# Reordering the opening, attention's last steps and the last stage's first block in a fused conditioned transformer block

## What is computed

```
# layer 0
shift, scale, gate = split(silu(t) @ ada_w + ada_b, 3)
norm = where(mask, layernorm(x) * (1 + scale) + shift, 0)
mlp  = gelu(norm @ ssm_w1 + b1) @ ssm_w2 + b2      # and the same with bwd_*; both summed
x    = x + gate * where(mask, mlp, 0)
x    = x + gate_mlp * (gelu_tanh(mod(layernorm(x)) @ ff_w1 + b) @ ff_w2 + b)
# layer 1
x    = x + attention(mod(layernorm(x)))            # 16 heads of 32, 128 x 128 scores
x    = x + (gelu(mod(layernorm(x)) @ w1 + b1) @ w2 + b2)   # hidden 2048
```

## Time and profile before

| | us |
|---|---|
| median of 3 runs (lowest, highest) | 1960.13 (1960.12, 1961.02) |
| the profiled execution's own time | 1960.09 |
| its span, first to last instruction | 1958.3 |

### The profile page before, as it was taken

How to read it: one execution, slowest core, us unless ns; L and a number is a source line. 1 busy time by engine, 2 the same in 40 slices (tenths; PEclk the granted TensorE clock), 3 DMA queues, 4 the chain that set the end, 5 groups by cost and what they waited for, 6 DMA issues and landing times.

```text
span 1958.3 us, 33154 instructions
## 1 busy us (share of the span) xinstructions
PE 1902.1 (97%) x11210; PEld 1573.8 (80%) x11210; DVE 1226.1 (63%) x2058; ACT 717.5 (37%) x2106; POOL 481.6 (25%) x577
## 2 busy tenths in 40 slices
PE   5999999999999999999999998899999999999999
PEld 4778888887888887888888886678888888888887
DVE  6577777766777765888888888445252534436222
ACT  3222232332232233777777776322121212122111
POOL 4333333322222222334443442101010101002000
PEclk8999999999999999999999999899999999999999
DMA  8545444444445443777777877512020111102000
GB/s 291 202 153 173 152 149 155 156 143 140 156 155 167 165 146 99 231 246 259 254 249 246 263 252 253 178 49 87 1 87 23 63 48 37 64 21 85 0 22 22
DMA packets 225104, 276.40 MB, mean 141 GB/s; under 512 B 15212, under 2 KB 144840, under 8 KB 225032
## 3 DMA queue, kind: packets, MB, share of 16 engines
q1 hardware_dynamic: 210712, 232.16, 35.8%
q0 software_dynamic: 12160, 39.14, 6.5%
q10 hardware_dynamic: 2160, 4.20, 0.6%
HBM read 175.29 MB, written 100.14 MB: 141 GB/s over the span
## 4 chain that ended last, share of the span: by engine, by line
PE 85%; DMA 6%; DVE 4%; issue 2%; ACT 1%; SPq 1%; POOL 1%; ACTq 0%; DVEq 0%; POOLq 0%
PE wide L657 33%; PE banks L634 32%; PE banks L1426 16%; PE wide L1459 2%; DMA turned_squares<-rows 2%; PE spare L1482 2%; DMA rows<-gate_bias_rows 1%; DMA rows<-turned_squares 1%; DMA x_tiles<-turned_probs 1%; DVE rows L893 1%; DMA rows<-in_L_cond_w_dram 1%; DMA turned_probs<-probs_room 0%; ACT probs_room L1621 0%; DVE weights L948 0%; DVE h L920 0%
## 5 line engine op out<-in xcount | busy, mean ns | idle before, releaser
L657 PE MATMUL wide<-weights,h 128*128 128x512 f32 x3072 | 758.8, 397 | 13.2 <-DVE h L920 13.2
L634 PE MATMUL banks<-xn,weights 128*128 128x512 f32 x3048 | 734.2, 391 | 5.6 <-DVE xn L908 5.6
L657 PEld LDWEIGHTS wide<-weights,h 128*128 128x128 f32 x3072 | 578.5, 189 | 155.4 <-DVE h L920 14.3
L634 PEld LDWEIGHTS banks<-xn,weights 128*128 128x128 f32 x3048 | 573.4, 188 | 130.7 <-DVE xn L908 6.0
L791 ACT ACTIVATE rows<-banks,vecs 128x512 f32<-128x512 f32 x256 | 176.4, 689 | 938.6 <-PE banks L634 928.4
L918 DVE CAST h<-rows 128x512 fp32r<-128x512 f32 x256 | 118.9, 464 | 441.0 <-ACT rows L791 439.7
L1426 PE MATMUL banks<-xn,weights 128*128 128x256 f32 (+1 forms) x1524 | 194.9, 289 | 0.7 <-DVE xn L1738 0.7
L1426 PE MATMUL banks<-weights,xn 128*128 128x512 f32 x780 | 189.5, 399 | 5.9 <-DVE xn L1785 5.9
L780 ACT ACTIVATE rows<-rows,mod_tables 128x128 f32<-128x128 f32 x360 | 148.4, 483 | 122.4 <-DMA rows<-turned_squares 121.6
L1426 PEld LDWEIGHTS banks<-xn,weights 128*128 128x128 f32 x1524 | 188.9, 193 | 4.8 <-DVE xn L1738 1.1
L920 DVE TENSOR_TENSOR h<-rows,h 128x512 fp32r<-128x512 f32 x256 | 185.1, 723 | 8.8
(11 more groups left out here) (132 smaller groups left out, 1491.0 us busy)
## 6 DMA issues: line engine op xcount, KB each, us to landing
turned_squares<-rows SPq DMA_DIRECT2D x124, 256.0 KB, 2.8
rows<-turned_squares SPq DMA_DIRECT2D x124, 256.0 KB, 2.9
turned_probs<-probs_room SPq DMA_DIRECT2D x62, 512.0 KB, 3.3
x_tiles<-x SPq DMA_DIRECT2D x98, 256.0 KB, 3.3
x<-x_tiles SPq DMA_DIRECT2D x96, 256.0 KB, 3.5
rows<-gate_bias_rows POOLq DMA_DIRECT2D x64, 256.0 KB, 4.0
probsT_room<-turned_probs SPq DMA_DIRECT2D x64, 256.0 KB, 4.1
x_tiles<-turned_probs SPq DMA_DIRECT2D x64, 256.0 KB, 4.9
```

The lines of the kernel that those rows point to most:

```text
L634: last = nc.tensor.matmul(m1_bank(c), st.tiles[0](a, k, c), xn[:, parity, b, k, :], start=s == 0, stop=s == len(steps) - 1)
L657: last = nc.tensor.matmul(y_ps[:, tile, :], h[:, c % 2, a, tile * P:(tile + 1) * P], st.tiles[1](b, c), start=c == 0 and s == 0, stop=c == ...
```

## The change

In the opening SP loads the tokens before the condition weights, and the weights in eight slices of 128 rows, each with a semaphore that PE waits for as it gets to it. The 15 vectors are loaded from ACT's queue. PE turns the first two token tiles and the vectors ahead of the condition product. DVE normalises all four tiles ahead of the table and splits the first weight pieces ahead of the tokens; POOL splits two pieces and then waits until the tokens are split. In block 0 of the first stage POOL asks for weight piece 2 between the fourth bias row's load and its addition, not behind the addition.

In attention's pair 0 DVE takes the row maxima before it splits the value bias, and SP alternates store and load of the squares. In the last steps SP loads the last pair's first half of probabilities and stores the second before it loads the squares; the store and the residual load of tile 1 go to the end. DVE does `finish(14, 0)` behind the row maxima and `finish(14, 1)` behind the output's split. ACT modulates before it copies the output. PE weighs the last tile between the two chunks ahead.

In the last stage's first block PE runs two first products ahead, in three banks; the last of them uses the bank of the old order. Pieces are split in the steps of `STEP_PIECES`: two in chunk 0, one in each of chunks 1 to 4, two in each of chunks 5 to 9. SP loads three token tiles ahead of the first pieces. One semaphore is made lasting, which changes no order.

```diff
@@ -277,7 +279,10 @@
         y_ps = sh.wide
-        m1_bank = lambda c: sh.banks[:, c % 2, :]
+        in_long_lead = lambda n: second_half_first and isinstance(n, int) and n == 0
+
+        def m1_bank(n, c):
+            return sh.banks[:, c % 3 if in_long_lead(n) and c < chunks - 1 else c % 2, :]
@@ -319,6 +324,9 @@
         LATE_LOAD_STEPS = {1: (2, 3), 3: (4, 5)}
+        STEP_PIECES = [(0, 1), (2,), (3,), (4,), (5,), (6, 7), (8, 9), (10, 11), (12, 13), (14, 15)]
+        step_of_piece = [c for c, pieces in enumerate(STEP_PIECES) for q in pieces]
+        own_pieces = lambda n, c: STEP_PIECES[c] if in_long_lead(n) and c < len(STEP_PIECES) else ()
@@ -379,13 +387,11 @@
                     sp.dma_start(cond, t["cond"]).then_inc(cond_loaded, 16)
-                    load_ada(0)
-                    load_ada(1)
...
                         load_x(stages[0], 0, 0, tile)
-                    for vec_name, (row, count) in VEC_ROWS.items():
-                        vector = t[vec_name][0:count * P].rearrange("(c p) -> c p", p=P)
-                        sp.dma_start(vec_rows[row:row + count, :], vector).then_inc(vec_loaded, 16)
+                    for k in range(KC):
+                        for n in range(2):
+                            sp.dma_start(room.weights[n][:, k, :], ada_items[n][k * P:(k + 1) * P, :]).then_inc(slice_loaded[k], 16)
@@ -396,13 +402,15 @@
                     sp.wait_ge(sh.cleared, 1)
+                    sp.wait_ge(sh.stored["att"][0], 16 * NPAIR)
+                    load_x(stages[0], 1, 1, 0)
+                    sp.wait_ge(*sh.values_read)
+                    for tile in range(TPP):
+                        load_x(stages[0], 1, 1, TPP + tile)
...
                         load_own_piece(q)
-                    for tile in range(TPP):
-                        sp.wait_ge(sh.stored["att"][tile], 16 * NPAIR)
-                        load_x(stages[0], 1, 1, tile)
-                    for tile in range(TPP):
-                        load_x(stages[0], 1, 1, TPP + tile)
+                    sp.wait_ge(sh.stored["att"][1], 16 * NPAIR)
+                    load_x(stages[0], 1, 1, 1)
@@ -415,11 +423,12 @@
                             for q in range(STAGE_RING, len(st.prefetch)):
-                                if tile == max(0, (q - STAGE_RING) // 2 - STATS_STEP + 1):
+                                if step_of_piece[q - STAGE_RING] == tile:
...
                             swap_squares(1, tile)
-                        for q in range(STAGE_RING + 2 * (TPB + STATS_STEP - 1), len(st.prefetch)):
-                            load_own_piece(q)
+                        for q in range(STAGE_RING, len(st.prefetch)):
+                            if step_of_piece[q - STAGE_RING] >= TPB:
+                                load_own_piece(q)
@@ -555,12 +564,12 @@
                 pool.wait_ge(zeroed, 2)
-                rstd_of(0, 0)
-                rstd_of(0, 1)
+                for tile in range(TPB):
+                    rstd_of(0, tile)
                 first_low(1)
-                rstd_of(0, 2)
-                rstd_of(0, 3)
-                for q in range(3, len(first_pieces), 2):
+                first_low(3)
+                pool.wait_ge(xn_ready, TPB)
+                for q in range(5, len(first_pieces), 2):
@@ -590,9 +599,11 @@
                         rstd_of(n + 1, tile + 1)
+                    if room and n == 0 and tile == TPB - 1:
+                        load_piece(stages[0], 2)
...
                 if not second_half_first:
-                    if n + 1 < total:
+                    if n + 1 < total and not (room and n == 0):
@@ -617,7 +628,14 @@
                     pe.wait_ge(xn_ready, ln(TPB * (n + 1)))
-                if not (isinstance(n, int) and n == 0 and c < 2):
+                if in_long_lead(n):
+                    if c == chunks - 1:
+                        pe.wait_ge(act_done, c - 1)
+                    elif c >= 3:
+                        pe.wait_ge(act_done, c - 2)
+                    else:
+                        pe.wait_ge(*sh.products_read)
+                elif not (isinstance(n, int) and n == 0 and c < 2):
@@ -661,9 +679,11 @@
-            def pair_product(out, cond_in, weights):
+            def pair_product(out, cond_in, weights, by_slices=False):
                 for k in range(KC):
+                    if by_slices:
+                        pe.wait_ge(slice_loaded[k], 32)
@@ -689,9 +709,10 @@
             def ada_product(out, pair):
-                pe.wait_ge(ada_loaded[2 * pair], 16)
-                pe.wait_ge(ada_loaded[2 * pair + 1], 16)
-                pair_product(out, room.silu, room.weights[2 * pair:2 * pair + 2]).then_inc(products_done, 1)
+                if pair:
+                    pe.wait_ge(ada_loaded[2 * pair], 16)
+                    pe.wait_ge(ada_loaded[2 * pair + 1], 16)
+                pair_product(out, room.silu, room.weights[2 * pair:2 * pair + 2], by_slices=pair == 0).then_inc(products_done, 1)
@@ -702,24 +723,28 @@
                 nc.tensor.transpose(cond_ps[:, P:P + B], mask_f, sh.ident[0:B, 0:B]).then_inc(mask_turned, 1)
+                first_turn(0)
+                first_turn(1)
+                pe.wait_ge(vec_loaded, 16 * len(VEC_ROWS))
+                nc.tensor.transpose(vec_ps[:, 0:N_VEC], vec_rows[0:N_VEC, :], sh.ident[0:N_VEC, 0:N_VEC]).then_inc(vec_turned, 1)
...
                 ada_product(item_ps, 0)
-                pe.wait_ge(vec_loaded, 16 * len(VEC_ROWS))
-                nc.tensor.transpose(vec_ps[:, 0:N_VEC], vec_rows[0:N_VEC, :], sh.ident[0:N_VEC, 0:N_VEC]).then_inc(vec_turned, 1)
...
                     opening()
-                    for tile in range(TPB):
+                    for tile in range(2, TPB):
...
             def block_step(n, parity, before, st, after):
-                first_product(st, n, parity, 0)
+                lead = 2 if in_long_lead(n) else 1
+                for c in range(lead):
+                    first_product(st, n, parity, c)
                 for c in range(chunks):
-                    if c + 1 < chunks:
-                        first_product(st, n, parity, c + 1)
+                    if c + lead < chunks:
+                        first_product(st, n, parity, c + lead)
@@ -818,28 +843,29 @@
                     act.dma_start(mask_u8[:, :], t["mask"]).then_inc(mask_loaded, 16)
+                    for vec_name, (row, count) in VEC_ROWS.items():
+                        vector = t[vec_name][0:count * P].rearrange("(c p) -> c p", p=P)
+                        act.dma_start(vec_rows[row:row + count, :], vector).then_inc(vec_loaded, 16)
...
                     nc.scalar.activation(room.silu, room.cond, ACT.Silu).then_inc(silu_done, 1)
-                    first_high(0)
-                    first_high(1)
...
                     for tile in range(TPB):
+                        first_high(tile)
                         modulate(stages[0], 0, tile)
-                        if tile in (1, 2):
-                            first_high(tile + 1)
...
                 for c in range(chunks):
-                    if second_half_first and isinstance(n, int) and n == 0 and 2 * c < len(st.prefetch):
-                        for q in (2 * c, 2 * c + 1):
-                            piece_high(st, n, q, st.prefetch[q][1], q % STAGE_RING, q // STAGE_RING)
+                    if in_long_lead(n) and c + 1 < chunks:
+                        activate(st, n, c + 1)
+                    for q in own_pieces(n, c):
+                        piece_high(st, n, q, st.prefetch[q][1], q % STAGE_RING, q // STAGE_RING)
...
                         first_high(11 + 2 * c)
-                    if c + 1 < chunks:
+                    if not in_long_lead(n) and c + 1 < chunks:
@@ -983,10 +1009,10 @@
             def first_table_rows():
+                dve.wait_ge(vec_turned, 1)
+                nc.vector.tensor_copy(sh.vecs[:, :], vec_ps[:, 0:N_VEC]).then_inc(vecs_done, 1)
...
                 nc.vector.tensor_copy(rows, item_ps[:, 0:HALF_D]).then_inc(rows_copied, 1)
-                dve.wait_ge(vec_turned, 1)
-                nc.vector.tensor_copy(sh.vecs[:, :], vec_ps[:, 0:N_VEC]).then_inc(vecs_done, 1)
@@ -1018,18 +1044,14 @@
                         stats(stages[0], 0, 0, tile)
+                    for tile in range(TPB):
+                        normalise(stages[0], 0, 0, tile)
                     first_table_rows()
-                    normalise(stages[0], 0, 0, 0)
                     make_first_table()
-                    normalise(stages[0], 0, 0, 1)
-                    normalise(stages[0], 0, 0, 2)
-                    split_xn(0, 0, 0)
-                    normalise(stages[0], 0, 0, 3)
-                    split_xn(0, 0, 1)
                     first_low(0)
-                    split_xn(0, 0, 2)
                     first_low(2)
-                    split_xn(0, 0, 3)
+                    for tile in range(TPB):
+                        split_xn(0, 0, tile)
@@ -1051,9 +1073,8 @@
```

(28 more changed lines are left out.)

20 lines of the change are left out of this document (12 added, 8 removed).

## The result

The changed kernel takes 1950.91 us (median of five runs, 1947.45 to 1952.47), the kernel before 1960.13; the ratio is 0.9947, with a 95% interval of 0.9937 to 0.9958. That is 9.2 us less where I forecast 16.4: the sign and the range hold, the size doesn't. The profiled execution is the one of 1950.91, its span 1949.1, so the two profiled executions differ by 9.2 us too and can be compared place by place. The ratio goes by all executions of a series; by it the gain is 10.4 us (8.2 to 12.3). Later series of the kernel before, on other chips of this kind, lie between 1956.3 and 1965.5, with medians of 1959.3 to 1961.9. One program on one chip spreads over up to 9 us, so single experiments are compared by their ratios and intervals, and the mechanism is read from the traces.

What follows compares the result with a forecast made beforehand. TensorE, busy 97% of the span, was taken as the bound, gains only where it idles or clocks low: -1.0 - 5.6 + 0 - 4.4 - 5.4 = -16.4, from 1960.1 to 1943.7 us; range 1937 to 1953.

Steps and rivals of the forecast that it cites:

- Opening: Until the first product: tokens loaded first bring it to 28.1 to 28.2 from 29.16, -1.0 us (bounds -2.0 to +1.0).
- Border: Blocks 0 and 1: earlier weight piece 2 cuts PE's idle gap and keeps the clock up, -5.6 us (bounds -3.3, -6.2).
- The clock's 2.3 us: Border of blocks 0 and 1: 12 matmuls no longer run at 1.2 instead of 2.4 GHz, 2.3 us of gain.
- Attention's first pair: Row maxima earlier, but exponentials still wait behind modulate of tile 1: 0 us (bounds -1.1 and +0.5).
- Attention's end: Last pair: probabilities loaded 3.0 us earlier, chunk 1 covers copy and split: -4.4 us (bounds -2.0 and -6.0).
- Rival 2: Attention's end: loads contend with stores, not brought forward; -2.0 for -4.4, whole 1946.1; chance 0.08 outside the forecast's band.
- Last stage: First block: two first products ahead, fewer pieces a step, less idle PE: -5.4 us (bounds -2.4 and -7.5).
- rival 1: Last stage's pieces 0 and 1 land late as today; clock still falls at the border: -11.1, 1949.0; chance 0.17.
- The slower rival: Opening: vector loads wait behind SP's bulk until about 33; table +20, less 15.4 elsewhere: 1964.7 us; chance 0.04.

Runs made afterwards that it cites:

- x_bestv: x_best with the vectors' transpose and copy put back behind the condition product: 1940.09 us, ratio 0.9901.
- x_best: Changed kernel plus four edits: last stage's pieces early, old opening split order, late weights held behind squares, late tables behind block 1's second rstd: 1940.11 us, ratio 0.99.
- x_order: Changed kernel with the old order of splits on ScalarE and VectorE between first table and first product: 1946.72 us, ratio 0.992.
- x_squares: Changed kernel with ScalarE's second pair of late weights held until the squares of block 1's tile 1 have landed: 1949.43 us, ratio 0.9955.
- attention alone: Kernel before with only the new attention orders (first pair and last steps): 1956.07 us, ratio 0.9978.
- x_bias: x_best with block 0's first bias load asked for ahead of weight piece 1: 1938.78 us, ratio 0.989.
- x_tables: Changed kernel with POOL's late tables and their store moved behind the first bias load of block 1: 1950.44 us, ratio 0.9944.
- x_pieces: Changed kernel with the last stage's first four weight pieces asked for ahead of attention's last residual load and last two stores: 1945.05 us, ratio 0.9915.
- opening alone: Kernel before with only the opening's part of the change: 1960.25 us, ratio 0.9997.
- border alone: Kernel before with only the next stage's weight piece 2 asked for ahead of the fourth bias add: 1958.44 us, ratio 0.9987.
- last stage alone: Kernel before with only the last stage's part: two first products ahead, pieces over ten steps, three token tiles loaded first: 1956.38 us, ratio 0.9977.
- x_weights: Changed kernel with ScalarE's issue of the second late-weight pair written behind the modulate of block 1's tile 0: 1951.1 us, ratio 0.9943.

## Why the prediction was right or wrong

**Opening** (forecast -1.0, measured nothing). The term that failed is the last vector: it landed at 12.8, inside the bounds that I gave (9 to 13.7) but not under 12.05, where I took it; the product started at 13.18, not 12.4, and the table was at 18.1, not 17.15. Even that was not all it hung on: x_bestv doesn't wait for the vector, and its product ends only 0.3 us earlier than that of x_best. Token tile 2 landed only at 7.1, where I had all four by 6.2, but that cost nothing, for the second turn ended at 12.14. The chain behind the table I had right: 11.0 forecast (17.15 to 28.15), 11.3 measured. I had worked out that the new order makes it as long as before and did not ask what it would be with the old one, which x_order shows: 8.2. A failing of the method, which cost nothing here as there was no gain: I let the opening's gain move all behind it ("whatever is won at those places moves all behind it"). In the traces it doesn't. The border 70 us later hangs on POOL's chain of bias rows, not on PE; of x_order's 2.3 us 0.5 get through, and nothing of the wait at 70.

On the queues: the last load of 2 KB on ScalarE's queue, behind the mask and 14 other vectors, still took from 7.2 to 12.8, 5.6 us, near the 6.42 of the earlier trace rows and far from the 2.1 of the earlier trace rows; that queue had little ahead of it, SP's had 3 MB under way. The squares' load, too, is delayed by weights that another queue asked for (x_squares). The Trainium skill, "DMA: Bandwidth & Descriptors", "Issuing engines are not separate DMA queues", says that another issuer saves only the sequencer's time. Both loads agree with it.

**The wait at 70** stood nowhere in the prediction. It is a race of two requests, SP's for 256 KB of squares and ScalarE's for 2 MB of late weights, 0.4 to 0.7 us apart. The change does not cause it: attention alone, which has the opening of before, waits there too (1.09 at 69.63). Of the four kernels with the old opening that one has the wait, of the six with the new one and nothing held five have it. It costs 1.3 us there and nothing at the border.

**Border** (forecast -5.6; alone -2.5 measured, -2.1 by the trace at the seventh chunk). The clock's 2.3 us came as forecast. The gap was mis-sized: I had the fourth bias landing as before, at 92.7, and it landed at 93.8 (5.5 us for 4.26), since piece 2 runs beside it: from the request until POOL masks the row it takes 5.0 to 5.8 us in nine of the ten kernels with the edit (3.9 in x_bias) and 4.4 to 4.6 in the four without it; so DVE's finish ended 1.0 later; and I had 0.62 for the subtraction and 1.1 for the split, which took 0.8 and 1.5 beside POOL's late tables, that in the kernel before were over by then. That is the 1.7 us by which the second product is later than my 97.5. And then about 2 us are given back in block 1: DVE's chain starts only 0.6 us earlier than before (it waits 1.8 for the rstd behind the tables, where it waited 0.8; I had allowed "under 0.5" for this), and its splits of h end 5.8, 6.1, 5.8 and 6.3 us behind one another where PE needs 5.53: 1.9 us too long in sum, so PE's 3.9 us of lead run into them. I had read the border by PE's wait and not asked how far ahead of DVE PE may get. x_tables shows that this later place for the tables alone does not mend that. Between the border's second product and that of the seventh chunk there are 40.4 to 40.7 us in all six kernels that keep the clock and have the tables where they were, wherever the border is; seven chunks of 5.53 would be 38.7.

**Attention's first pair** (0; -0.2 in the changed kernel and -0.3 in attention alone up to the next scores, +0.1 in x_pieces and x_tables). Right. PE waits 1.4 us less for the exponentials (2.77, before 4.17), but 0.90 for the value bias, now split later, stands ahead of it; ScalarE starts the modulate of tile 1 only 0.2 us sooner behind the scores (2.9, before 3.1).

**Attention's end** (-4.4; -4.1 in the changed kernel, -3.2 alone, -4.8 in x_pieces). Right, by its mechanism: the weighing starts 2.5 us sooner behind the last scores (12.3, before 14.8; forecast 3.0), ahead chunk 1 covers the wait before the last projection. Rival 2 is out.

**Last stage** (-5.4; -3.6 in the changed kernel, -4.1 alone). My own places give -5.8: second product 6 7.5 us earlier and first product 8 of 2.8 done, less the 4.4 of attention's end; I had added up PE's idle times to 8.9 where the starts give 9.8. What failed is rival 1's first half; its second, a lower clock at the border, did not come. The term is the landing of the pieces: I took the 4.64 of the earlier trace rows and had piece 0 there at 1246.0, 10.3 behind the start of the last projection. It was issued at 1240.52 and split at 1246.81, 6.3 us later and 12.4 behind that start. The token tiles beside the pieces took the width: with three of them ahead, the first piece takes 5.6 to 6.3 us in six traces, and 4.0 to 5.0 in the four that ask for the pieces first. So second product 1 was at 1249.94, with 3.28 of idle for 1.05. The two waits behind it, 0.39 and 0.80, are near the 0.6 and 1.05 forecast. x_pieces shows the missing 1.8 us and 3.2 more: my bounds ran from the order that the change wrote, and SP could ask for the pieces 18 us earlier.

**The slower rival** (vectors behind the bulk until 28.5) did not come near: 12.8.

Sum: forecast -1.0 - 5.6 + 0 - 4.4 - 5.4 = -16.4; measured from place to place 0 - 2.0 (+0.9 of scatter up to 751) - 0.5 (from 751 to the last scores, 0.2 of it at the first pair) - 4.1 - 3.5 = -9.2. So the time fell inside the range because attention's end came as forecast, the border gave 2 of its 5.6 and the last stage two thirds. The measured 1950.9 lies in the band of rival 1 (1948 to 1954), and that its 1949.0 is so near is partly luck: it had 1.0 from the opening and a clock that falls at the border, neither of which is there, and nothing given back in block 1.

## What to carry to other kernels

A gain at one place counts only as far as the next place that hangs on another chain. Before summing gains, walk from each to the next wait of the bounding engine and ask which engine or queue released it, and since when that chain has been running: here, in the traces, a chain of four loads on POOL swallowed nearly all that was won or lost in the 70 us ahead of it, until both the opening and the squares were earlier. When a wait is removed on the bounding engine, look at how long the steps of the engine behind it are, for a lead runs into steps that are longer than its own. And an early request is cheap where a queue stands idle and the buffer is free: moving four loads 18 us forward won 5.0 us on top of the 3.6 of the lead of two products.

## What the hardware showed

- **The order of two requests goes with 2 to 3 us of a load.** The squares' 256 KB took 6.7 to 7.5 us when asked for 0.43 to 0.53 us behind the start of the issue of two 1 MB loads of another queue (the second is issued 0.5 us behind the first; four traces), and 9.3 to 9.8 when asked for 0.61 to 0.67 behind it (six traces). With the weights held back until they have landed, 2.8. That the weights cost the load some 4 to 7 us is shown by holding them back; that a tenth of a microsecond decides between 7 and 9.5 is read from ten traces, and no edit set that distance.
- **The clock falls after some gaps and not after longer ones.** PE's 12 matmuls behind a gap, in us. Windows of 4 or 5 us that begin with them show a granted 1.00 (2.4 GHz) for those of 3.0 to 3.1, and for the longer ones 0.50 (before, border) to 0.68, which is a mean of both levels:

```
gap    12 matmuls   kernel, where
1.93      4.58      opening alone, second product 0 of the last stage
1.93      3.03      border alone, the same place
1.94      4.57      before, the same place
1.94      3.03      attention alone, the same place
2.05      4.47      last stage alone, second product 1
2.29      3.06      x_squares, border
2.36      3.06      border alone, border
2.50      4.61      attention alone, last stage
2.74      3.06      x_order, last stage
3.20      4.61      attention alone, border
3.28      3.06      changed kernel, last stage
3.94      5.27      before, border
4.09      4.61      last stage alone, border
4.18      4.34      opening alone, border
```

  At the border the gaps up to 2.36 kept the clock and those from 3.20 on lost it. In the last stage length does not order them, and the same gap of 1.93 at the same place went either way. What else decides stays open.
- **ScalarE's queue issues DMAs ahead of the activations before them** (56.41 against 56.92 in x_weights). Behind a wait for a semaphore the same request was held, until 59.69 (x_squares). So moving a request behind an activation in the program did not delay it here; a wait did.
- **VectorE beside POOL.** DVE's subtraction of 128x512 took 0.88 us beside POOL's late tables (changed kernel) and 0.68 without them (x_tables), the cast of h 0.68 for 0.42.
